# The last tiles of an attention and mixture-of-experts kernel: a written-out order for each engine, three bias sums on VectorE, and 768 tokens summed on chip

## The reference

```python
x = gamma * out + x                       # out: attention of each pixel row against the image, from 1x1 q, k, v
t = to_tokens(x)                          # [4, 1024, 256]
t = t + ln(t) @ W1 + (memory @ ln(t)) @ W2 + bias    # memory: band of 32 earlier tokens, entry i - j
u = ln(t)
sel = sigmoid(u @ expert_sel.T)           # 32 experts; the two best of each token
h = relu(einsum('td,edh->teh', u, keys))
t = t + einsum('teh,te,ehv->tv', h, w, values)       # w: the two best values of sel, else 0
```

## Time and profile before

| | us |
|---|---|
| median of 3 runs | 504.38 (503.53 to 505.4) |
| the profiled execution, its own time | 505.53 |
| its span in the profile | 503.8 |
| tile loop (energies of tile 0 to the last tiles' first steps) | to about 277 |
| drain and plan | 277 to 319.5 |
| groups | 319.5 to 475.5 |
| closing sums and end | 475.5 to 503.8 |

### The profile page before, as it was taken

The page is one execution under the profiler, slowest core; times in us unless marked ns, Lnnn a source line. Parts: engine busy times, 40 slices in busy tenths (PEclk is TensorE's granted clock), DMA queues, the critical chain, the costliest instruction groups (busy, mean ns, idle before and its releaser), DMA issues.

```text
span 503.8 us, 10424 instructions
## 1 busy us (share of the span) xinstructions
PE 397.0 (79%) x3007; PEld 307.7 (61%) x3007; DVE 335.9 (67%) x1022; ACT 283.6 (56%) x828; POOL 297.1 (59%) x386
## 2 busy tenths in 40 slices
PE   8879999999999999999999775759686757467000
PEld 3557778777878788787778563338464546356000
DVE  1856688987879787899999536536566678478000
ACT  1144767766767676778787455248655676354000
POOL 5333546766677777678888656343566655446700
PEclk9999999999999999999999857698989879799655
DMA  6998001411111111111111111476554443331195
GB/s 208 312 213 190 25 12 37 133 45 43 55 44 54 45 43 54 34 55 54 56 65 44 43 44 54 119 247 193 167 166 130 128 138 105 107 101 45 11 208 114
DMA packets 28441, 49.58 MB, mean 98 GB/s; under 512 B 6204, under 2 KB 21966, under 8 KB 27373
## 3 DMA queue, kind: packets, MB, share of 16 engines
q1 hardware_dynamic: 20512, 26.72, 20.0%
q0 software_dynamic: 7872, 22.19, 14.3%
HBM read 30.77 MB, written 25.73 MB: 112 GB/s over the span
## 4 chain that ended last, share of the span: by engine, by line
PE 48%; SPq 17%; issue 13%; DVE 11%; DMA 3%; ACT 2%; POOL 2%; POOLq 0%; DVEq 0%; ACTq 0%
PE bank L1234 21%; SPq L412 8%; PE bank L1196 7%; SPq L409 5%; PE bank L1128 5%; PE bank L1217 4%; PE bank L1224 3%; DVE vT L803 2%; SPq L276 2%; PE bank L1110 2%; DVE z_lo L818 2%; DMA biasb<-bias 2%; PE bank L1208 1%; PE X L1196 1%; SPq L277 1%
## 5 line engine op out<-in xcount | busy, mean ns | idle before, releaser
L1234 PE MATMUL bank<-vT,prob 128*128 128x256 f32 x512 | 116.0, 380 | 0.7 <-DVE vT L803 0.7
L580 POOL DMA_INDIRECT out<-vT,dest x80 | 78.5, 981 | 64.3 <-DVE vT L1062 42.7
L1234 PEld LDWEIGHTS bank<-vT,prob 128*128 128x128 f32 x512 | 94.9, 190 | 13.4 <-issue 1.1
L510 POOL TENSOR_TENSOR prob<-prob,ginv 128x1024 f32<-128x1024 f32 x32 | 61.3, 1916 | 25.9 <-DVE ginv L905 25.8
L487 POOL DMA_INDIRECT slot_rows<-rows,slot x64 | 64.8, 1013 | 16.2 <-issue 16.2
L481 POOL TENSOR_TENSOR rstd<-rstd,half_neg 128x1 f32<-128x1 f32 x64 | 36.0, 562 | 57.4 <-ACT rstd L632 56.1
L747 ACT ACTIVATE prob<-X 128x512 f32<-128x512 f32 x40 | 22.3, 593 | 50.9 <-remote 19.5
L691 ACT ACTIVATE prob<-prob 128x1024 f32<-128x1024 f32 x32 | 33.9, 1059 | 22.7 <-DVE prob L878 22.7
L1062 DVE SCALAR_TENSOR_TENSOR vT<-bank,wgt,vT 128x256 f32<-128x256 f32 x80 | 33.2, 478 | 16.0 <-remote 9.5
L874 DVE TENSOR_REDUCE gmax<-X 128x32 f32<-128x1024 f32 x32 | 39.2, 1224 | 5.9 <-PE X L1159 5.8
L899 DVE TENSOR_REDUCE gsum<-prob 128x32 f32<-128x1024 f32 x32 | 38.8, 1212 | 4.4 <-ACT prob L691 4.3
(11 more groups left out here) (203 smaller groups left out, 907.8 us busy)
## 6 DMA issues: line engine op xcount, KB each, us to landing
xc_or_xin<-slot_rows SPq DMA_DIRECT2D x32, 130.0 KB
xt<-x_tok SPq DMA_DIRECT2D x32, 128.0 KB, 2.1
values_s<-values SPq DMA_DIRECT2D x2, 2048.0 KB, 29.5
out<-out POOLq DMA_DIRECT2D x4, 1024.0 KB, 14.6
xc_or_xin<-x_cm SPq DMA_DIRECT2D x3, 1024.0 KB, 21.8
t<-slot_rows SPq DMA_DIRECT2D x16, 130.0 KB
t<-slot_rows SPq DMA_DIRECT2D x32, 65.0 KB
xc_or_xin<-slot_rows SPq DMA_DIRECT2D x32, 65.0 KB
```

What stands on the lines that cost most here:

```text
L510: g.tensor_tensor(prob[:, t % 2], prob[:, t % 2], ginv[:, t % 2].unsqueeze(2).to_broadcast([P, WT * KB, W]), ALU.mult).then_inc(prob_done, 1)
L580: g.indirect_dma_start(out=out, out_offset=bass.IndirectOffsetOnAxis(ap=dest[:, n % (2 * NB), k:k + 1], axis=0), in_=yb[:, n % NB, k, :], ...
L1234: mm = m.matmul(av_p, pr[:, j, :], vT[:, b % 2, j, :], start=(j == 0), stop=(j == KB - 1))
```

## The change

Four things are changed.

1. The drain loops are replaced by a list of steps for each of PE, DVE, ACT and POOL. `attend(31)` comes first on PE. `mix(29)` and `mix(30)` follow one another, the steps of tiles 30 and 31 are taken apart, `route` is split into its parts, and on POOL the scatters stand between the factors of the layer norms. The matmuls on unused data are 3 and 3.
2. `t1b` has three buffers in place of two, and in the drain the bias sums of tiles 29, 30 and 31 are made on DVE (`last_bias`), not on POOL.
3. The accumulating DMAs cover 3328 rows. The other 768 rows (`TAIL_ROWS` = 6 on each of 128 partitions) are loaded from both halves into SBUF, one half by SP and one by ACT, each 768 KB, as soon as `y_sent` allows.
4. DVE adds them in two instructions, and SP and ACT store 384 KB each once the additions are done and the accumulating DMAs have landed (`stored`).

```diff
+TAIL_ROWS = 6
+IN_PLACE = N - TAIL_ROWS * P
-DRAIN_WARM = 6
+DRAIN_WARM = 3
...
-        t1b = sb("t1b", [P, 2, C])
+        t1b = sb("t1b", [P, 3, C])
...
+            for i in range(NB):
+                sp.wait_ge(y_sent[i], sent_before(GROUPS))
+            sp.dma_start(tail[:, 0], tail_rows(0)).then_inc(ld_tail[0], 16)
+            sp.wait_ge(tail_added, 1)
             sp.wait_ge(stored, 16 * SUMS)
+            sp.dma_start(tail_rows(0)[:, tail_half(0)], tail[:, 0, tail_half(0)]).then_inc(tail_stored, 16)
+            sp.wait_ge(tail_stored, 32)
...
-                after(pool, t2_done, t - 1)
-                g.tensor_tensor(t1b[:, t % 2], t1[:, t % 3], biasb[:, :], ALU.add).then_inc(t1b_done, 1)
+                after(pool, t2_done, t - 2)
+                g.tensor_tensor(t1b[:, t % 3], t1[:, t % 3], biasb[:, :], ALU.add).then_inc(t1b_done, 1)
...
+            send(NT - 8)
+            first_factors(NT - 2)
+            send(NT - 7)
...
-            sums_d = out.rearrange("(r c n k) e -> r c n (k e)", r=2, c=SUMS, k=SUM_ROWS)
+            sums_d = [out[r * N:r * N + IN_PLACE, :].rearrange("(c n k) e -> c n (k e)", c=SUMS, k=SUM_ROWS) for r in range(2)]
             for c in range(SUMS):
-                g.dma_start(sums_d[0, c], sums_d[1, c], accum_op=ALU.add,
+                g.dma_start(sums_d[0][c], sums_d[1][c], accum_op=ALU.add,
...
+            a.dma_start(tail[:, 1], tail_rows(1)).then_inc(ld_tail[1], 16)
+            act.wait_ge(tail_added, 2)
+            act.wait_ge(stored, 16 * SUMS)
+            a.dma_start(tail_rows(0)[:, tail_half(1)], tail[:, 0, tail_half(1)]).then_inc(tail_stored, 16)
...
+            def last_bias(t):
+                dve.wait_ge(t1b_done, NT - S_MIX)
+                dve.wait_ge(t1_done, t + 1)
+                after(dve, t2_done, t - 2)
+                v.tensor_tensor(t1b[:, t % 3], t1[:, t % 3], biasb[:, :], ALU.add).then_inc(t1b_done, 1)
...
+            for r in range(2):
+                dve.wait_ge(ld_tail[r], 16)
+            for i in range(2):
+                v.tensor_tensor(tail[:, 0, tail_half(i)], tail[:, 0, tail_half(i)], tail[:, 1, tail_half(i)],
+                                ALU.add).then_inc(tail_added, 1)
```

More of the change, by code:

```diff
@@ L267, in attention_moe @@
         stored = sem("stored")
+        ld_tail, tail_added, tail_stored = [sem(f"ld_tail{r}") for r in range(2)], sem("tail_added"), sem("tail_stored")
         def after(eng, s, n):
@@ L532, in _, with first_row, second_row @@
                                     ALU.subtract).then_inc(w_lo_done, 1)
[L534 to L551, removed]
+            def first_row(t):
+                rows_complete(t)
+                scatter_rows(t, 0)
+            def second_row(t):
+                scatter_rows(t, 1)
+            send(NT - 8)
+            first_factors(NT - 2)
+            send(NT - 7)
+            first_row(NT - 6)
+            first_factors(NT - 1)
+            second_factors(NT - 4)
+            second_row(NT - 6)
+            second_factors(NT - 3)
+            send(NT - 5)
+            second_factors(NT - 2)
+            send(NT - 4)
+            second_factors(NT - 1)
+            send(NT - 3)
+            send(NT - 2)
+            send(NT - 1)
             pool.wait_ge(u2_copied, 2 * GROUP * P // C)
@@ L715, in _ @@
                     first_squares(t)
[L717 to L740, removed]
+            turned(NT - 3)
@@ new lines, in _ @@
+            columns_written(NT - 6)
+            second_copy(NT - 5)
+            first_norm(NT - 2)
+            first_squares(NT - 1)
+            second_squares(NT - 4)
+            turned(NT - 2)
+            second_turned(NT - 5)
+            z_high(NT - 3)
+            z_high(NT - 2)
+            logits_exp(NT - 5)
+            first_norm(NT - 1)
+            second_norm(NT - 4)
+            second_squares(NT - 3)
+            turned(NT - 1)
+            second_turned(NT - 4)
+            columns_written(NT - 5)
@@ L933, in route, with best_places @@
                 v.max(top[:, t % 4], sig[:, t % 2]).then_inc(top_done, 1)
+            def best_places(t):
                 dve.wait_ge(top_done, t + 1)
                 v.max_index(topi[:, t % 2], top[:, t % 4], sig[:, t % 2]).then_inc(topi_done, 1)
[L936 to L954, removed]
-                for t in tiles(s, S_TURN):
-                    turned_low(t)
@@ L957, in _ @@
-            slots(NT - 1)
+            def last_bias(t):
[3 more added lines that the diff above has]
+                v.tensor_tensor(t1b[:, t % 3], t1[:, t % 3], biasb[:, :], ALU.add).then_inc(t1b_done, 1)
+            z_low(NT - 4)
+            turned_low(NT - 3)
+            place_rows(NT - 7)
+            chosen(NT - 6)
+            both_chosen(NT - 6)
+            last_bias(NT - 3)
+            last_bias(NT - 2)
@@ new lines, in _ @@
+            first_sum(NT - 1)
+            second_sum(NT - 4)
+            last_bias(NT - 1)
+            place_rows(NT - 6)
+            turned_low(NT - 2)
+            z_low(NT - 3)
+            z_low(NT - 2)
+            plus_one(NT - 5)
+            second_sum(NT - 3)
+            sigmoid(NT - 5)
+            two_best(NT - 5)
+            best_places(NT - 5)
+            chosen(NT - 5)
+            both_chosen(NT - 5)
+            turned_low(NT - 1)
+            place_rows(NT - 5)
+            second_sum(NT - 2)
@@ new lines, in _ @@
+            plus_one(NT - 4)
+            sigmoid(NT - 4)
+            two_best(NT - 4)
+            best_places(NT - 4)
+            chosen(NT - 4)
+            both_chosen(NT - 4)
+            z_low(NT - 1)
+            place_rows(NT - 4)
+            second_sum(NT - 1)
+            plus_one(NT - 3)
+            sigmoid(NT - 3)
+            two_best(NT - 3)
+            best_places(NT - 3)
+            chosen(NT - 3)
+            both_chosen(NT - 3)
+            place_rows(NT - 3)
+            plus_one(NT - 2)
```

108 lines of the change are left out of this document (82 added, 26 removed).

## The result

The changed kernel took **497.12 us** (median of 4 runs, 495.73 to 497.48) beside 504.48 for the kernel before (median of 4, 503.53 to 505.4): ratio 0.9849, 95% interval 0.9823 to 0.9875, so 7.4 us faster where the prediction had 9.8. The profiled execution took 497.05 us with a span of 495.2.

The account below looks back on a forecast made before the run. The chain was taken to run over PE's tile loop for about half the span, then SP's issue of row loads. Drain 9.4 + end 0.4 = 9.8 us off 504.38 gave 494.6 us; range 491 to 500 (own range 493 to 496.5).

Parts of the forecast that it names:

- the drain's chain: Drain, from POOL's last scaling at 279.19 through attend(31) to the last slots: they end at 305.0, 9.4 us earlier.
- the walk: Drain steps timed one by one from the timelines: last slots at 304.7, clock low from 299.5 on, 0.3 us short.
- the bound of 25.7 us: Drain on POOL from 279.19: 16 scatters and six pairs of factors, so it can't end before 304.9.
- the clock doesn't fall midway: Drain: PE's clock stays high to about 294; the rival fall midway gives back 2.5 to 4.5 us, 497 to 499, chance 0.18.
- Plan, loads and groups hang on the slots and move along: Stages behind the drain: they start earlier with the last slots; last result row lands at about 466.
- the sum: Whole kernel: 9.4 us from the drain and 0.4 from the end, together 9.8 us faster.
- the end: Closing stage: adding DMAs -3.8 us, tail loads +3.7, 0.5 hidden, stores +0.2; net -0.4, from -3.8 to +4.4.
- what hides beside the slow start: Closing stage: tail loads start beside the adding DMAs' slow start (share 0.39), which hides 0.5 us.
- the +0.2: Closing stage: both stores take 3.9 to 4.1 us beside the DRAIN's 4.1, so 0.2 us shows.
- Loads that overlap for free: Rival at the end: loads and adding DMAs overlap inside the DMA engines, -3.8 us, 491.2 us; chance 0.12.
- Loads at 229 GB/s: Rival at the end: loads run at 229 GB/s and stores stick out behind the DRAIN, +4.4 us, 499.4; chance 0.12.
- The slow plain transfers that would have made it slower: Rival at the end: plain transfers starve beside adding ones at 62 GB/s, +11.5 us less 9.4, 506.5; chance 0.04.

Follow-up runs that it names:

- the attention later: Changed kernel with attend(31) moved back on PE to just ahead of mix(29): 465.83 us beside 468.59 for the kernel before, ratio 0.9935.
- the attention first alone: Kernel before with only attend(31) moved to the front of the drain on PE: 465.70 us beside 467.79, ratio 0.9953.
- slow issue made by hand: Unused offset reads added on SP ahead of row loads: kernel before 468.14 us (ratio 1.0005), changed kernel 458.70 (0.9796), both beside 467.79.
- the stores beside them: Changed kernel with the tail's two stores no longer waiting for the adding DMAs: 461.36 us beside 468.42 for the kernel before, ratio 0.9840.

## Why the prediction was right, and where not

**Right: the drain's chain.** Forecast were the attention at 279.2 (279.10), the last slots at 305.0 (304.37), the clock at 1.00 to about 294 with its fall in the walk at 299.5 (298 to 300), and -9.4 us (-10.0 in the trace; -9.3 measured alone on chip 12). POOL nearly worked through, as the bound of 25.7 us said: it took 27.9 from 279.05 to its last scatter's end, at 306.99, where the walk had 307.0.

**Right: that the clock doesn't fall midway.** The experiments with the attention later and with the attention first alone show that both this order without the early attention and the early attention without this order run into it.

**Wrong: "Plan, loads and groups hang on the slots and move along".** The plan did; the groups gave back 2.9 us (some 4 by the medians), and the last result row landed at 468.4, not at about 466. I had read the earlier trace rows, where SP's queue has 17% of the chain, and taken the groups for a block of fixed length. They weren't: their issue ran in blocks of 12 or up to 25 us for 16 loads, and from first to last load it took 128.6 us in the one program and 131.4 in the other. On the two chips without the slow blocks the sentence holds (groups of 117.4 to 118.7 us in eleven of the twelve traces, 120.3 in one) and the whole change gives 9.6 us on one and 9.1 to 9.4 on the other, where the sum said 9.8. What stays open is whether the loss on the first chip is bound to the earlier start or is how the slow instructions happened to fall; only one trace of each kernel exists there, no run of the study landed there, and slow issue made by hand left no instruction.

**Right in part by luck: the sum.** 7.4 us came out for a forecast of 9.8 although a term of 2.9 was missing, because the drain and the end of the first chip's traces each gave more than forecast (0.6 and 1.1).

**Wrong in size: the end.** Forecast was -0.4. In the first chip's traces it is -1.5. By the medians of chip 12 the new end alone gives -1.0 (interval 0.3 to 1.9), and beside the new drain -0.1 (459.15 and 459.01), so the forecast isn't refuted there. The bytes came out as put: the mid-stage window of the changed kernel moved 213 GB/s and the mean over 476 to 490 is 209 (205 assumed), and one window with loads and adding DMAs together moved 412 (422 assumed for loads alone).

```profile
468.00:470.00 2.00, 0.00 (x0) 0.00 (x0) 0.00 (x0) 0.00 (x0) 0.95 (x2) 0.50 0.40 83
470.00:472.00 2.00, 0.00 (x0) 0.00 (x0) 0.00 (x0) 0.00 (x0) 2.00 (x4) 0.50 0.82 295
472.00:474.00 2.00, 0.00 (x0) 0.00 (x0) 0.00 (x0) 0.00 (x0) 0.60 (x1) 0.50 1.10 412
...
478.00:480.00 2.00, 0.00 (x0) 0.00 (x0) 0.00 (x0) 0.00 (x0) 0.00 (x0) 0.50 1.04 213
```

What I had too small was what hides beside the slow start. Behind the last row the adding DMAs of before had 24.0 us for 20.5 us of bytes, so 3.5 us of start. Now it is 22.6 for 16.6 + 3.7, so 2.3: the loads hide 1.2 us of it, not 0.5. The window of the earlier trace rows with its share of 0.39 begins 0.46 us behind the last landing; the same window of the changed kernel, 468.86 to 470.86, has 0.70. On the other chips the same two times are 23.2 to 23.5 us (four traces with the old end) and 22.4 to 22.6 (six with the new one and 768 tokens): about 0.9 less, so the loads hide some 0.8 us there, and a part of the 1.5 is that the one trace of before was long at this place. The stores took 3.3 us instead of 3.9 to 4.1, and lie beside the DRAIN in full: the +0.2 doesn't show.

**The rivals.** Loads that overlap for free: out, the end fell by 1.5, not 3.8, and the stores beside them showed what bytes cost. Loads at 229 GB/s: out. The slow plain transfers that would have made it slower: out, the loads landed in 6.8 and 7.5 us. Its sum was off by a little too: 515 less 503.7 is 11.3, not 11.5, and so 506.3; and in the walk two scatters at 1.26 are 2.52, not 2.55. Neither changes the forecast.

## What to carry to other kernels

Walk a short serial stretch through its steps with durations from the trace, and let each step's clock level be part of the walk: an order pays twice when it fills the wait in which the clock would fall, and half of such an order may be worth a quarter of the whole or less (2.1 and some 1.8 of 9.3 us here). Before you let a stage "move along", look whether equal pieces of it take equal time; where 16 equal loads take 12 us here and 25 there, a head start ahead of it may not be passed on in full. Bytes taken off the slowest transfer are worth their difference in rate, plus what starts early enough to run in that transfer's own slow start.

## What was unexpected of the hardware

- **SP's register instructions can be 20 times as long.** In the first pair they, or the gaps between them, took 0.72 us in stretches, in the twelve runs on two chips hardly ever; the 112 row loads cost 117 to 124 us of issue against 85 to 87. The groups are 34 us shorter without it in the kernel before. Why is not known.
- **How much a change is worth depends on where it runs.** The same pair of programs differs by 7.4 us (ratio 0.9849, 0.9823 to 0.9875) in one place and by 9.6 (0.9789, 0.9770 to 0.9808) on chip 12; the intervals don't meet, and in us (6.3 to 8.9, and 9.0 to 10.8) they just miss each other.
- **A closing DRAIN on POOL** ended 3.97 or 3.98 us behind the last landing of its adding DMAs in all fourteen traces, which hides two stores of 384 KB (3.3 us).
